# Edge stage of a graph network: VectorE adds the gathered row of one step in four, tiles turned three batches ahead, PSUM buffers four deep

## What is computed

```python
# 50000 nodes, 50000 edges, 128 features; L = 2 layers; dst is sorted and dense at low node numbers
x = layernorm(x + graph_conv(x, src, dst))
h = x @ W_enc.T + b_enc
for l in range(2):
    m = concat([h[src], h[dst]])
    m = relu(m @ msg_W1[l].T + msg_b1[l])
    m = m @ msg_W2[l].T + msg_b2[l]
    agg = segment_sum(m, dst)
    h = layer_norm(h + concat([h, agg]) @ upd_W[l].T + upd_b[l])
x = layernorm(x + h @ W_out.T + b_out)
```

## Time and profile before

| What | Value |
|---|---|
| runs | 3439.77, 3447.5, 3446.47 us |
| profiled execution | 3446.32 us, its span 3444.6 us |
| granted clock of TensorE, mean of the span | 0.971 |
| busy of the span: TensorE, VectorE, ScalarE, GpSimd | 86%, 78%, 69%, 54% |
| first matmul to last chained sum, first layer's edge stage | 1587.8 to 2119.0 us |
| the same, second layer | 2542.3 to 3074.2 us |

### The profile page before, as it was taken

One profiled execution on the slowest core, in us unless ns is written; L12 is line 12 of the kernel. 1 busy time (PEld: TensorE's weight loads), 2 busy tenths in 40 slices (PEclk: granted clock), 3 DMA queues, 4 the chain that ended last, 5 costly groups with the idle time before them and its releaser, 6 DMA issues. The chain is left out here.

```text
span 3444.6 us, 92529 instructions
## 1 busy us (share of the span) xinstructions
PE 2975.2 (86%) x25312; PEld 2674.1 (78%) x25312; DVE 2700.0 (78%) x8634; ACT 2379.7 (69%) x5642; POOL 1846.0 (54%) x1782
## 2 busy tenths in 40 slices
PE   4975656777767789997999998999979999989998
PEld 3753334555543378987999998999979999989998
DVE  9999967888856688885777776666657777769998
ACT  3779945777742368886777775666657777759999
POOL 0000036577755533335776776555547767766664
PEclk9999988999979989999999999999989999999999
DMA  0027635777649989997776654999977766548887
GB/s 21 2 69 229 223 103 162 221 219 215 195 139 340 346 280 355 366 356 250 225 221 208 191 158 123 327 327 326 328 239 229 221 210 194 164 129 287 296 295 240
DMA packets 460711, 777.79 MB, mean 226 GB/s; under 512 B 113689, under 2 KB 115865, under 8 KB 460393
## 3 DMA queue, kind: packets, MB, share of 16 engines
q1 hardware_dynamic: 355046, 548.85, 48.2%
q10 hardware_dynamic: 67714, 147.73, 12.5%
q0 software_dynamic: 37632, 77.15, 9.2%
HBM read 451.50 MB, written 321.78 MB: 224 GB/s over the span
## 5 line engine op out<-in xcount | busy, mean ns | idle before, releaser
L883 DVE SCALAR_TENSOR_TENSOR edges_acc<-edges_acc,keep,edges_ps_a 128x128 f32 (+1 forms) x2352 | 820.3, 349 | 272.1 <-issue 145.9
L851 POOL DMA_INDIRECT ring<-table_p,esrc x784 | 787.5, 1004 | 313.3 <-issue 206.0
L1011 PE MATMUL edges_ps_m<-ring,ident 128*128 x3136 | 609.7, 276 | 33.8 <-POOLq L840 33.8
L1012 PE MATMUL edges_ps_m<-edges_q_ring,edges_turned 128*128 x3136 | 608.8, 276 | 0.0
L1011 PEld LDWEIGHTS edges_ps_m<-ring,ident 128*128 128x128 f32 x3136 | 478.6, 193 | 34.7 <-ACT edges_turned L967 17.7
L1012 PEld LDWEIGHTS edges_ps_m<-edges_q_ring,edges_turned 128*128 128x128 f32 x3136 | 478.8, 193 | 0.0
L979 ACT ACTIVATE edges_msg<-edges_ps_m 128x512 f32<-128x512 f32 x392 | 234.2, 597 | 295.5 <-PE edges_ps_m L1012 294.7
L1021 PE MATMUL edges_ps_a<-edges_onehot,edges_msg 128*128 128x128 f32 x3136 | 414.0, 275 | 0.0
L851 POOL DMA_INDIRECT ring<-table_h,esrc x344 | 327.7, 953 | 138.5 <-issue 93.5
L1021 PEld LDWEIGHTS edges_ps_a<-edges_onehot,edges_msg 128*128 128x128 f32 x3136 | 381.7, 192 | 0.0
L868 DVE TENSOR_TENSOR edges_onehot<-iota,drel 128x512 f32<-128x512 f16 x441 | 305.0, 692 | 96.1 <-PE edges_ps_a L1021 94.0
(11 more groups left out here) (315 smaller groups left out, 6776.2 us busy)
## 6 DMA issues: line engine op xcount, KB each, us to landing
table_z<-nodes_z_t SPq DMA_DIRECT2D x196, 256.0 KB, 5.0
table_p<-nodes_p_out SPq DMA_DIRECT2D x196, 256.0 KB
table_q<-nodes_q_out ACTq DMA_DIRECT2D x196, 256.0 KB
edges_q_ring<-table_q SPq DMA_DIRECT2D x196, 256.0 KB, 4.8
edges_d_ring<-table_d ACTq DMA_DIRECT2D x98, 512.0 KB
table_t<-edges_acc SPq DMA_DIRECT2D x196, 256.0 KB
nodes_in_a<-table_t SPq DMA_DIRECT2D x196, 256.0 KB
nodes_in_z<-table_z SPq DMA_DIRECT2D x196, 256.0 KB, 4.3
```

What stands on the lines that cost most here:

```text
L851: nc.gpsimd.indirect_dma_start(out=ring[:, e % RE * W:e % RE * W + P], out_offset=None, in_=table[:, :], in_offset=bass.IndirectOffsetOnAx ...
L883: nc.vector.scalar_tensor_tensor(out=to, in0=to, scalar=m.keep[:, s:s + 1], in1=ps_a[:, i % AR, where(j):where(j) + F], op0=ALU.mult, op1= ...
L1011: nc.tensor.matmul(to, m.ident[:], rows[j], start=True, stop=False)
L1012: last = nc.tensor.matmul(to, turned[:, i % QR, j * P:(j + 1) * P], slots[j], start=False, stop=True)
```

## The change

Of the four steps of a batch, the first (`ADDED = 1`) no longer gets TensorE's product with the identity. Its `turned` product starts the PSUM tile, and VectorE adds the gathered rows to it in place (`add_rows`), before ScalarE's activation. ScalarE and GpSimd wait for the new semaphore `s_added` where they waited for `s_pq`. Tiles are turned `LEAD = 3` batches ahead instead of two, and QR is 4 instead of 3. add_rows(i - 1) stands at the head of VectorE's round i, and reads four words of `m.steps` in every second batch.

```diff
--- before.py
+++ after.py
@@ -28,12 +28,13 @@
 RE = 64
 RC = 8
 RG = 4
-HR, QR, BEHIND = 3, 3, 2
+HR, QR, BEHIND = 3, 4, 2
 XR = 4
 HELD = 0
 RING = 4
 DB, DR = 4, 3
 SHARE = 4
+ADDED, LEAD = 1, 3
 PRE = 48
 W = P + J
 EW = -(-NCHUNK // 3)
@@ -779,7 +780,7 @@
         if not degrees:
             turned, msg = sb("turned", [P, QR, CH]), sb("msg", [P, QR, CH])
             d_ring = sb("d_ring", [P, DR, DB * CH], F16)
-            ps_m = pb("ps_m", 512, QR)
+            ps_m, s_added = pb("ps_m", 512, QR), sem("s_added")
         else:
             xin, x_t, r_out = sb("xin", [P, XR, CH]), sb("x_t", [P, 2, CH]), sb("r_out", [P, XR, CH])
             ps_x, ps_r = pb("ps_x", 512, 1), pb("ps_r", 512, 1)
@@ -844,7 +845,7 @@
                         k = g - RE // 4
                         if k % 24 == 0:
                             ends = load(mybir.EngineType.Pool, m.tile_end[0:1, k // 3:k // 3 + 8])
-                        pool.wait_ge(s_seg if degrees else s_pq, third(ends, k))
+                        pool.wait_ge(s_seg if degrees else s_added, third(ends, k))
                         pool.sem_inc(s_go, 1)
                     for j in range(4):
                         e = 4 * g + j
@@ -860,7 +861,7 @@
             def _(dve):
                 nc.vector.memset(acc[:], 0.0).then_inc(s_zero, 1)
                 dve.wait_ge(s_zero, 1)
-                slots = {}
+                slots, word = {}, {}
 
                 def hot(i):
                     if i >= HR:
@@ -883,6 +884,18 @@
                         nc.vector.scalar_tensor_tensor(out=to, in0=to, scalar=m.keep[:, s:s + 1], in1=ps_a[:, i % AR, where(j):where(j) + F],
                                                        op0=ALU.mult, op1=ALU.add).then_inc(s_chain, 1)
 
+                def add_rows(i):
+                    if i % 2 == 0:
+                        word[0] = load(mybir.EngineType.DVE, m.steps[0:1, 2 * i:2 * i + 4])
+                    rows = [ring[:, bass.ds(word[0][i % 2 * 2] // (1 << (7 + 6 * j)) % RE * W, P)] for j in range(ADDED)]
+                    for at in rows:
+                        nc.vector.lower_ap(at)
+                    dve.wait_ge(s_pq, i + 1)
+                    for j in range(ADDED):
+                        to = ps_m[:, i % QR, j * P:(j + 1) * P]
+                        last = nc.vector.tensor_tensor(to, to, rows[j], ALU.add)
+                    last.then_inc(s_added, 1)
+
                 def relu_x(c):
                     dve.wait_ge(s_res, c + 1)
                     if c >= XR and c % RING != HELD:
@@ -892,6 +905,8 @@
 
                 lag = 2 if degrees else BEHIND + 1
                 for i in range(NB + (lag + 2 if degrees else lag)):
+                    if not degrees and 1 <= i < NB + 1:
+                        add_rows(i - 1)
                     if i < NB and (not degrees or i % SHARE == SHARE - 1):
                         hot(i)
                     if lag <= i < NB + lag:
@@ -968,12 +983,12 @@
 
                     for g in range(DR - 1):
                         load_drel(g)
-                    turn(0)
-                    turn(1)
+                    for i in range(LEAD):
+                        turn(i)
                     for i in range(NB):
-                        if i + 2 < NB:
-                            turn(i + 2)
-                        act.wait_ge(s_pq, i + 1)
+                        if i + LEAD < NB:
+                            turn(i + LEAD)
+                        act.wait_ge(s_added, i + 1)
                         if i >= QR:
                             act.wait_ge(s_seg, i - QR + 1)
                         nc.scalar.activation(msg[:, i % QR, :], ps_m[:, i % QR, :], ACT.Relu).then_inc(s_msg, 1)
@@ -1002,14 +1017,15 @@
 
                 def combine(i):
                     landed = due(i)
-                    rows, slots = addressed([row(i, j) for j in range(4)]), addressed([slot(i, j) for j in range(4)])
+                    rows, slots = addressed([row(i, j) for j in range(ADDED, 4)]), addressed([slot(i, j) for j in range(4)])
                     pe.wait_ge(s_turned, 2 * i + 2)
                     pe.wait_ge(s_prow, landed[0])
                     pe.wait_ge(s_n, landed[1])
                     for j in range(4):
                         to = ps_m[:, i % QR, j * P:(j + 1) * P]
-                        nc.tensor.matmul(to, m.ident[:], rows[j], start=True, stop=False)
-                        last = nc.tensor.matmul(to, turned[:, i % QR, j * P:(j + 1) * P], slots[j], start=False, stop=True)
+                        if j >= ADDED:
+                            nc.tensor.matmul(to, m.ident[:], rows[j - ADDED], start=True, stop=False)
+                        last = nc.tensor.matmul(to, turned[:, i % QR, j * P:(j + 1) * P], slots[j], start=j < ADDED, stop=True)
                     last.then_inc(s_pq, 1)
 
                 def segment(i):
```

## The result

The changed kernel took 3467.1 us, the median of 4 runs (3465.1 to 3471.6), beside 3443.6 for the kernel before (4 runs, 3439.8 to 3447.5): a ratio of 1.0073, interval 1.0060 to 1.0087. It is slower by 23 us, where 74 were forecast.

A forecast was written before the change was run, and what follows sets the result against it. TensorE bounds the edge stages now; VectorE would become the bound at 2.87 us a batch against 2.68, losing 75 us over 392 batches. 3446.3 + 75 = 3521, said as 3520 us; range 3418 to 3575.

The forecast's parts named there:

- VectorE becomes the bound: Edge stages: VectorE's round rises to 2.87 us a batch against 2.68, losing 75 us; chance 0.62.
- the message: Sign in the layers: TensorE at 85%, its idle time put down to waiting for the message.
- Addition, address, and hiding: VectorE's round without a read: addition 0.285 us, one address 0.235, four addresses (0.94) hidden under addition and one-hot; 2.385 us.
- The price of the four-word read: VectorE's table read before every second addition: 0.80 us, making the addition 0.775 us late and that round 3.16 us.
- the lower bound, 0.62: Low end for the four-word read's price, taken from the short kind of eight-word reads on VectorE; the high end was 1.37.
- Reads by the word, the first rival: VectorE's four-word read costs half of eight: 0.31 us gives 3420 us, 0.40 no change; chance 0.26.
- the point of decision: Price of one VectorE read at which the first rival decides: 0.41 us.
- Reads slow each other: Rival: five table reads in eight batches replace one and contend; all at 1.37 us gives 3662, half way 3571; chance 0.08.
- The main case: VectorE is the new bound in the edge stages; about 3520 us, own range 3475 to 3575, chance 0.62.
- GpSimd's floor of 3420 us: Untouched gathers, 1.007 + 0.30 us each, leave only 26 us to gain in both layers, whatever TensorE saves.
- TensorE's clock: Rival: idling 15% of each batch lowers the clock; a tenth of both layers would cost 86 us more; chance 0.02.
- Buffers at nothing: Four PSUM buffers and tiles turned three ahead, including the prologue's third tile (1.43 us of ScalarE), count as nothing.

The follow-up runs named there:

- z13: Changed kernel with the address computed every batch from words read once, pointing into a constant tile; one gathered row in four missing from the output: 3390.0 us, ratio 0.9851.
- z12: Changed kernel with one table word read in every batch instead of four in every second: 3533.5 us, ratio 1.0275.
- z11: Changed kernel with the added row's read and address, and the read of slots, moved between VectorE's chained sums: 3391.9 us, ratio 0.9846.
- x1: Changed kernel with no row added by VectorE and all twelve products on TensorE, keeping the deeper buffers and lead of three: 3441.4 us, ratio 0.9997.
- z14: z11 with two rows of four added by VectorE (ADDED = 2): 3376.4 us, ratio 0.9817.
- x2: Changed kernel adding a constant tile instead of gathered rows, without table read or address; output lacks one row in four: 3387.6 us, ratio 0.9840.
- z7: Changed kernel with three buffers and tiles turned two batches ahead, as before the change: 3474.7 us, ratio 1.0103.
- x3: x2 with the four-word read of steps kept in the code but unused; the read never ran on the chip: 3392.1 us, ratio 0.9848.
- x6: Changed kernel reading eight neighbouring words every fourth batch instead of four every second, on a slower chip: 4068.7 us, ratio 1.0177.
- x5: Changed kernel reading four words at a stride of two every fourth batch, instead of four neighbours every second: 3494.8 us, ratio 1.0149.

## Why the prediction was right or wrong

- **VectorE becomes the bound: right, but by less than was said.** Its one-hot waits no more for TensorE, its idle time is its own issue, and ScalarE and GpSimd wait for the addition. TensorE was to be at 85% in the layer; it is at 95.5% there. That the page says 85% is another number, for the whole span, and was 86 before. Its idle time is put down to the turned tiles and not, as forecast, to the message.
- **Addition, address, and hiding: right in size.** The addition is 0.296 us, 0.285 was taken; the next operation starts 0.20 us after it, not 0.285. The four addresses (0.94) are then no longer fully covered, so that one-hot to sums is 0.80 us. The two offset each other: 2.41 us for a round, 2.385 forecast. z13 shows the address for free.
- **The price of the four-word read: wrong, and this is the step that failed.** "The two nearest prices, 0.62 and 1.37 for eight words, are the ends; I take their mean by count, 0.80." Measured: 0.385 us in 75 of 92, so the addition is 0.36 us late, not 0.775. That is 4 x 0.41 = 1.7 us too much in eight batches, and the lower bound, 0.62, was none. TensorE's read in the earlier trace rows was rightly called the nearest, but one occurrence stood for all, and its length was inferred from a gap. The trace of before has that read by itself: 0.699 us, a long one. The median of TensorE's 93 four-word reads in the first layer is 0.332 us. Both rows stand above. The price that the forecast lacked could have been read before any run.
- **Reads by the word, the first rival: right in its number, wrong in its cause.** It gave 0.31 or 0.40 for four words, "no change" at 0.40, and 0.41 as the point of decision. The measured 0.385 put into the prediction's own sum gives 19.08 + 4 x 0.36 + 0.80 = 21.3 us, against 21.42: no change. That the kernel came out slower, as forecast, is therefore partly luck: what tips it are rounds of 2.41 us and the longer ones among the reads, not the price that was taken. And z12 shows that there is hardly a price by the word from one to four.
- **Reads slow each other: not shown.** Some of the reads are indeed long (16 of 92 gaps, and 9 of 23), worth about 0.3 us in eight batches. The main case had them in its mean. What makes them long is open. In the changed kernel 9 of the 13 four-word reads over 0.42 us fall together with a table read of another engine, and 4 of the 79 others; but in z11 only 2 of 26 long ones do, and in the kernel before none of the 7 long reads of `slots`.
- **GpSimd's floor of 3420 us: wrong.** It took the gathers at 1.007 us, a mean. The median is 0.944 before and 0.944 to 0.948 in the versions since; what differs is how many are longer. These belong to VectorE's one-hot: of the 106 gathers that start up to 0.45 us after a one-hot has started, 98 take over 1.0 us in the kernel before, and of the 267 others 15. In x1, with TensorE's work as before, it is 137 of 138 and 15 of 234, and the mean rises to 1.032; in z14 it is 15 of 16 and 3 of 355, mean 0.956. The floor seems to have been set by where in the round the gathers fell; no run moved the one-hot to test it. Three programs (x2, z13, z11) ran at 3388 to 3392 us.
- **TensorE's clock: right.** It is granted 1.00 through 500 us at 95% busy. **Buffers at nothing: right** for the kernel before (x1); in the changed kernel z7 leaves some 10 us open.
- **The times.** 3467 lies inside 3418 to 3575, but just under the main case's own range, 3475 to 3575.

## What to carry to other kernels

Moving work from the full engine to one that is "78% busy" must also be priced in sequencer time: what the new operation has to read and compute before it can be handed over, and whether anything is queued ahead to cover that. If nothing is, do the read and the address one operation earlier, between operations that wait for each other anyway: here this turned 1.007 into 0.985 with the same arithmetic. Where only one price decides the sign, look for the instruction itself, all its occurrences and their median, before taking a mean of distant rows: here the row was in the trace of before. And before an experiment is read, count in its trace the instruction that it is about; x3's was not there.

## What the runs showed of the hardware

- A read of table words into VectorE's registers takes 0.309 us for one word (z12), 0.347 for four neighbours (changed kernel), 0.598 for eight (`slots`, x6), and 0.953 for four words a stride of two apart (x5), in the median. Some are longer, up to 0.753 us for four neighbours in the changed kernel and 1.329 for eight in the kernel before.
- Between sums that wait for one another, a read and an address cost no time that shows in the kernel's (z11). The sum behind a four-word read can start 0.04 us later than without (0.42 after the one before, instead of 0.38); VectorE had that slack.
- A gather on GpSimd takes 0.944 us in the kernel before. Nearly all the longer ones there, up to 1.44 us, start within 0.45 us of a one-hot on VectorE (98 of 113). Its mean is 1.007 us in the kernel before, 0.966 in x2 and 0.956 in z14.
- Two of the chips ran every kernel some 15 to 16% slower, with standstills of 2 us in the stages that are straight code. An order between versions measured there (z11's code slower than before by 1.8%) was the opposite of that on the other chips (faster by 1.5%).
